# A graph layer kernel: the last stage's index words in loads of 16 registers instead of 32, and two small operations earlier in a hop's end

## The reference: two graph layers, each with a norm behind it

```python
edge_index = jnp.stack([src, dst])
x = _layernorm(x + _L0_gnn_ref(x, edge_index, edge_attr_70, Wf, bf, Wq, Wk, Wa, Wu, bu), axis=-1)
x = _layernorm(x + _L1_gnn_ref(x, edge_attr3_4x1, src, dst), axis=-1)
```

```python
def f(y):
    return jax.ops.segment_sum(y[src3] * e3, dst3, num_segments=N)
k1 = f(x)
k2 = f(x + dt * k1 / 3)
k3 = f(x + dt * (k2 - k1 / 3))
k4 = f(x + dt * (k1 - k2 + k3))
y = x + dt * 0.125 * (k1 + 3 * (k2 + k3) + k4)
```

## Time and profile before

| | |
|---|---|
| median of 3 runs | 3495.34 us |
| the profiled execution | 3501.67 us |
| its span, first to last instruction | 3499.9 us |
| busy in the span: PE, DVE, ACT, POOL | 1189.6, 2478.0, 1452.2, 2597.1 us |
| the walk's stretch, about 3096 to 3500 us: busy PE, DVE, ACT, POOL | 304.3, 126.5, 127.4, 339.7 us |
| mean granted TensorE clock, span and walk | 0.627 and 0.83 |

### The profile page before, as it was taken

The page is one execution under the profiler, slowest core; times in us unless marked ns, Lnnn a source line. Parts: engine busy times, 40 slices in busy tenths (PEclk is TensorE's granted clock), DMA queues, the critical chain, the costliest instruction groups (busy, mean ns, idle before and its releaser), DMA issues.

```text
span 3499.9 us, 31921 instructions
## 1 busy us (share of the span) xinstructions
PE 1189.6 (34%) x6041; PEld 999.4 (29%) x6041; DVE 2478.0 (71%) x6241; ACT 1452.2 (41%) x3372; POOL 2597.1 (74%) x2761
## 2 busy tenths in 40 slices
PE   4666664666661311101111101111100000047777
PEld 4555653544441211101111101111000000046776
DVE  7677616888888786657777767777769999943332
ACT  4445544666661222213333323333325555533333
POOL 7777766777757777767777767777767777748888
PEclk8777787788875555555555555555555555568888
DMA  5555585666653444436777767777757777777775
GB/s 134 172 167 176 175 174 159 217 211 213 215 193 114 147 138 151 147 121 220 252 255 241 248 202 243 247 253 254 237 180 261 263 260 259 264 215 196 197 205 142
DMA packets 423033, 710.22 MB, mean 203 GB/s; under 512 B 100050, under 2 KB 286734, under 8 KB 416592
## 3 DMA queue, kind: packets, MB, share of 16 engines
q1 hardware_dynamic: 235754, 474.50, 40.0%
q0 software_dynamic: 82128, 182.11, 19.2%
q10 hardware_dynamic: 104960, 51.58, 5.1%
HBM read 370.71 MB, written 337.25 MB: 202 GB/s over the span
## 4 chain that ended last, share of the span: by engine, by line
POOL 43%; issue 17%; DVE 14%; PE 8%; DMA 2%; ACT 2%; ACTq 0%; DVEq 0%; SPq 0%; POOLq 0%
POOL gs L1573 32%; POOL gs L834 10%; PE psum L1937 8%; DVE psum L1689 3%; DVE stats L1239 2%; DVE tn L1654 2%; DVE da L1699 2%; DVE psum L1670 2%; DVE new_res L1233 2%; ACT psum L1632 1%; DVE mv L1245 1%; DMA gs<-u,far_row 0%; PE psum L1919 0%; DVE last_z L1695 0%; DMA u<-cross,first_idx 0%
## 5 line engine op out<-in xcount | busy, mean ns | idle before, releaser
L1573 POOL DMA_INDIRECT gs<-u,far_row x1176 | 1115.4, 948 | 363.6 <-issue 357.4
L1133 PE MATMUL psum<-wu_i,d_xt 128*128 128x128 f32 (+1 forms) x782 | 210.9, 443 | 1100.0 <-DVE d_res L1165 1099.9
L1632 ACT ACTIVATE psum<-da 128x512 f32<-128x512 f32 x288 | 173.1, 601 | 888.3 <-DVE tn L1654 553.8
L1670 DVE TENSOR_TENSOR psum<-gs,psum 128x1024 f32<-128x1024 f32 x192 | 234.9, 1224 | 419.0 <-DMA gs<-u,far_row 285.1
L1133 PEld LDWEIGHTS psum<-wu_i,d_xt 128*128 128x128 f32 (+1 forms) x782 | 176.4, 326 | 1136.4 <-issue 1136.4
L343 POOL DMA_INDIRECT pt<-in_x_dram,idx x392 | 386.1, 985 | 123.6 <-issue 119.0
L834 POOL DMA_INDIRECT gs<-rows_e,edge_id x392 | 370.9, 946 | 141.4 <-issue 119.1
L1573 POOL DMA_INDIRECT gs<-x1s,far_row x392 | 374.2, 955 | 120.7 <-issue 119.1
L1689 DVE TENSOR_TENSOR_SCAN psum<-goes_on,psum 128x1024 f32<-128x1024 f32 (+1 forms) x200 | 447.5, 2238 | 0.6
L1909 DVE TENSOR_TENSOR hot<-pos,rel_s 128x1536 f32<-128x1536 f32 x66 | 125.4, 1903 | 255.3 <-ACT psum L1975 228.1
L1937 PE MATMUL psum<-ring,hot 128*128 x1584 | 292.4, 340 | 11.0 <-issue 1.6
(11 more groups left out here) (286 smaller groups left out, 3944.4 us busy)
## 6 DMA issues: line engine op xcount, KB each, us to landing
u<-da SPq DMA_DIRECT2D x144, 512.0 KB, 4.0
rows_e<-pt SPq DMA_DIRECT2D x48, 1056.0 KB, 4.7
total<-tn SPq DMA_DIRECT2D x98, 512.0 KB, 3.3
gs<-total SPq DMA_DIRECT2D x98, 512.0 KB, 5.9
fin_d<-normed SPq DMA_DIRECT2D x49, 516.0 KB, 4.9
ring<-fin_d SPq DMA_DIRECT2D x49, 516.0 KB, 4.7
gs<-u SPq DMA_DIRECT2D x49, 512.0 KB, 5.4
gs<-x1s SPq DMA_DIRECT2D x49, 512.0 KB, 6.4
```

What stands on the lines that cost most here:

```text
L1133: t = pe.matmul(d_new_psum[k % 2][0:P, r * D:(r + 1) * D], d_xt[k % 4][:, r * 128:r * 128 + P], wu_i[:, :], start=True, stop=True)
L1573: g.indirect_dma_start(gx[b % 4][:, j * D:(j + 1) * D], None, source[:, :], bass.IndirectOffsetOnAxis(ap=far_row[:, c:c + 1], axis=0)).the ...
L1632: act.mul(shared, half(us[b % 3], i), share).then_inc(shared_set, 1)
L1670: return v.tensor_tensor(zf.rearrange("p (h f) j -> p j h f", h=H), by_head(gxv(b % 4)[:, c0:c1, 0:D]), per_head(wt_rest[:, c0:c1, :] if b ...
```

## The change

There are two edits.

1. WORDS, the number of steps for each load, goes from 24 to 12. A row of `place_d` and `place_s` is then PITCH = 12 + 4 = 16 words long, and PE loads 16 registers for each 12 steps, 66 times, in place of 32 registers for each 24 steps, 33 times. The total number of words stays 1056. SP writes 66 short rows into `place_d` instead of 33 longer ones, in the same two transfers.
2. In hop 3's end, `o_shifts(v, 47)` (the last batch but one) stands ahead of `keep_last` of the last piece instead of behind `o_rows(v, 48)`.

```diff
-WORDS = 24
+WORDS = 12
+PITCH = WORDS + WORDS // 3
@@
-    place_d = nc.dram_tensor("place_d", (STEPS // WORDS, 32), I32).ap()
+    place_d = nc.dram_tensor("place_d", (STEPS // WORDS, PITCH), I32).ap()
@@
-                sp.dma_start(place_d[:, WORDS:32].unsqueeze(0), at_open.rearrange("o (g k) -> o g k", k=WORDS // 3)
+                sp.dma_start(place_d[:, WORDS:PITCH].unsqueeze(0), at_open.rearrange("o (g k) -> o g k", k=WORDS // 3)
@@
                 add_up_runs(i + 1)
+                if h == 3:
+                    o_shifts(v, b - 1)
                 keep_last(i + 1)
@@
                     o_rows(v, b)
-                    o_shifts(v, b - 1)
                     o_statistics(v, b)
@@
-        place_s = sb("place_s", [1, STEPS // WORDS * 32], I32)
+        place_s = sb("place_s", [1, STEPS // WORDS * PITCH], I32)
@@
-                        place_s[0:1, 32 * n:32 * n + 32], (mybir.EngineType.PE,), min_val=0,
+                        place_s[0:1, PITCH * n:PITCH * n + PITCH], (mybir.EngineType.PE,), min_val=0,
@@
-                        g = n * 2 + tri // TRI_OF
+                        g = n * (WORDS // GROUP) + tri // TRI_OF
```

## The result

The changed kernel takes 3503.74 us, the median of 14 runs (3500.8 to 3511.17); beside it the kernel before took 3496.19 (3492.66 to 3499.3, 14 runs). The ratio is 1.0023, with a 95% interval of 1.0016 to 1.0030: some 7.6 us slower. The prediction said 3512 and slower.

A forecast was written before the change was run, and what follows sets the result against it. PE's sequencer, not its engine, was taken to bound the walk. Loads 15.6, walk's end 1, hop's end 0 and words' transfers 0 made 16.6 us, over the median of 3495.34 3511.9, said as 3512 us; range 3494 to 3518.

The forecast's parts named there:

- What bounds the walk: In the walk, PE's sequencer sets the pace, not its engine: 11.90 us a piece, 8 x 1.18 and a load.
- The load: In PE's walk, 65 loads of 16 registers on the path in place of 32 of 32: +15.6 us.
- L32: Time of one load of 32 registers in PE's walk, taken as 2.5 us.
- L16: Time of one load of 16 registers in PE's walk, put at 1.47 us.
- the line between the two prices that were measured: PE's load price: straight from 0.50 us for one register to 2.5 for 32; 8 to 19 us added, 66 in 100.
- The rival by the register: PE's loads priced by register alone, 1.25 us for 16: +1.3 us, 3497.6 with the walk's end; 16 in 100.
- The walk's end: Behind the walk's last load, four tris may run at a low clock: up to 1.4 us, put at 1.
- break-even: In the walk, the change costs nothing if a load of 16 registers takes 1.23 us.
- The slow clock as rival: In the walk, PE's clock stays at 1.2 GHz through all four tris: 12 us on top, 3524; 8 in 100.
- The hop's end: In hop 3's end, moving `o_shifts` to the scan's end changes nothing at the statistics: 0, 0.2 us either way.
- the words' transfers: SP's two transfers into DRAM in hop 0 may double their issue time, 1.8 us uncovered; put at 0.
- Two signs named in advance: In PE's timeline, pieces of 12 steps about 6.2 us apart, and waits on "issue" of 85 to 95 us.

The follow-up runs named there:

- E7: Kernel before with each step's product over 65 of its 129 columns, the other columns of the sums left out, loads and instructions as many: ratio 1.0006.
- E3: As E1, but a load of 8 registers for each 6 steps, 132 loads: ratio 1.0035, +12 us.
- E6: As E1, but each of the 66 loads takes 32 registers, of which 16 are used: ratio 1.0252, +87 us.
- E4: Kernel before with loads of 24 registers for each 24 steps, and the tri's own word by a one-register load at each of 264 tris: ratio 1.0258, +91 us.
- E5: As E3, but a load of 4 registers for each 3 steps, 264 loads: ratio 1.0154, +53 us.
- E1: The change without the moved `o_shifts`, so only the loads of 16 registers against the kernel before: ratio 1.0025.
- E2: Kernel before with only the `o_shifts` move in hop 3's end, loads still of 32 registers: ratio 1.0002.

## Why the prediction was right, and where its size was off

**What bounds the walk: right.** The sequencer's own time does. E7 (experiment 7) leaves the time as it was with 77 us more of engine work in the walk; E3 to E6 change only the loads, with the same products, and the time follows the loads; and in the changed kernel the pieces are 4 x 1.18 us and a load. One reading was off without harm: of the two waits on `hot` in the earlier trace rows only the 5.38 us at the start are `hot`. The other one, 2.77 us at 3174.56, is a load's: its `hot` was done at 3162.9.

**The load: the sign right, the size off.** The term was 65 x 1.47 - 80 = +15.6 us. It measured 65 x 1.355 - 78.7 = +9.4. L32 was 2.46 instead of 2.5, which is +1.3. The rest is L16. The step that was mis-sized is "the line between the two prices that were measured": one end, 0.50 us for one register, was ACT's 0.58 us with a guess at what the waits and the copy's start take of it. On PE one register costs 0.33 to 0.36 us. And the line is not straight. By size, undisturbed (the shortest that come often, less 1.17) and as a mean over the walk (the mean piece less 1.18 us for each tri):

| registers | shortest common, us | mean, us |
|---|---|---|
| 1 (E4) | 0.33 to 0.36 | not separated |
| 4 (E5) | 0.38 to 0.40 | 0.51 |
| 8 (E3) | 0.65 | 0.72 |
| 16 (after; E1) | 1.14 | 1.355; 1.31 |
| 32 (before; E2) | 2.20 | 2.46; 2.42 |

The last price stands in an interval before, from the eighth tri's open to the next piece's, 3.37 - 1.17:

```profile
3337.99 0.17 PE L1919 MATMUL psum<-none 128*128 128x2 bf16 x1
...
3341.36 0.17 PE L1919 MATMUL psum<-none 128*128 128x2 bf16 x1 [2.10 <-issue]
```

Undisturbed, from 4 registers on each further one costs some 0.065 us; from 1 to 4 they are almost free. So an undisturbed load of 8 or more pays about 0.12 us beside its registers, where the line had 0.44. In the means it is more, 2 x 1.355 - 2.46 = 0.25 us by the lengths 16 and 32. The first end of the line was a least price, and I had read it as a fixed part of every load. The rule of the Trainium skill that the prediction set beside it ("DMA: Bandwidth & Descriptors", "Latency and other measured facts", a floor of some 600 ns) has the word for this, a floor; its size was not met, a load of one register on PE taking 0.33 to 0.36 us; ACT's 0.58 us, which the prediction took as agreeing with it, was an upper bound that had waits and a copy's start in it. The other rule (the Trainium skill, "Runtime: NRT & Kernel Launch", "Instruction fetch mechanics", 200 ns for each register from HBM) has the form that the price takes from 4 registers on, at a third of its size for SBUF.

**The rival by the register** (+1.3 us) was nearer in its mechanism than in its number. Half of 2.46 is 1.23 us, and the load of 16 took 1.355: 0.125 us more for each of 65 loads, 8 of the 9.4 us. That is half of what a load costs beside its registers, since half of 2.46 has half of one such part in it. The other 1.2 us is the first load, which both kernels hide and which had 32 registers before.

**How much of this was luck.** The break-even was L16 = 1.23, half of L32. By undisturbed loads alone the change adds 65 x 1.14 - 32 x 2.20 = +3.7 us, within the 7 us that the prediction called no change. The other 5.7 of the 9.4 us come with the longer kind of load, which comes at every length that was measured and which the prediction did not know. That the slowdown came out above these 7 us rests on this longer kind. It also hid part of the error: the forecast fixed part, 0.44 us, was nearly four times the 0.12 us of undisturbed loads, and the longer loads, which it left out, made up for some of the difference.

**The walk's end: right as a risk, wrong as a sum.** I put 1 us for a slow clock behind the last load. The last four tris ran at 1.18, 1.17 and 1.15 us; from the last load's open to the span's end are 12.2 us after and 17.0 before, and four tris fewer are 4.7. It cost nothing here, because the clock in these last 4.6 us was 1.00. The case that the prediction feared is in E6's profile: behind its last load the granted clock was 0.54, the tris were 1.80, 1.54 and 1.53 us apart, and from the last load's open (3571.63) to the span's end (3585.2) are 13.6 us, 1.4 more than after. So the 1 us was a price that some executions can pay, not a wrong mechanism.

**The slow clock as rival: did not come.** The granted clock in the walk rose from 0.83 to 0.88, with shorter gaps, and the pieces that had tris at the slow clock are not longer than the others: the 26 pieces after in which some tris stood 1.5 us or more apart took 5.96 us in the mean, the other 39 took 6.15. The prediction's reason against this rival does not hold in general, though: in E7 PE had hardly a gap left, and the granted clock stayed at 0.50.

**The hop's end and the words' transfers: right.** 4.43 against 4.45 us, and E2's ratio; 0.85 and 1.01 us for the issues.

**Two signs named in advance.** Pieces of 6.2 us were said, and over 6.3 for the clock, 6.0 for a price by the register: 6.075 lies between. The waits on "issue" were to grow to 85 to 95 us and fell to 62.8. That forecast forgot what the earlier trace rows had shown, that a load beside a busy engine leaves no idle time.

**Left open.** Loads and some tris come in a second length, mostly 0.2 to 0.4 us longer (0.65 and 0.90 in E3, 1.14 and 1.49 after; a few loads after are 0.6 longer); it accounts for most of the gap between the two columns of the table. What causes it was not tested. It is not random: in E5 long and short intervals alternate over most of the walk (95 of the 109 that are over 1.7 us are at every second load), and in E3 the long load comes at every fifth load from the middle of the walk on, most with a tri of 1.3 us before it. Fetches of PE's instructions can't be all of it: E5's trace has 44 packets of instructions, for all engines together, between 3096 and 3541 us. No version here beats the kernel before: loads get cheaper for each word only as they get longer, and 32 registers is the longest that was tried.

## What to carry to other kernels

Where addresses come from registers, count the sequencer's time for a piece of work, loads included, from open to open, and not the engine's idle time beside it: in this walk that idle time fell while the time rose. Few long register loads beat many short ones, but by a small fixed part (0.12 us each for undisturbed loads here, some 0.25 us in the mean), so halving a load of 32 cost 9 us over 65 loads and not the 87 that as many full loads cost. And do not lay a line through the shortest case of an operation: what it costs at size one may be a least price that longer ones do not pay on top.

## What the runs showed of the hardware that was not expected

- A register load from SBUF on PE: 0.33 to 0.36 us for one register, 0.38 to 0.40 for four, 0.65 for eight, 1.14 for sixteen, 2.20 for thirty-two, where nothing disturbs it. Only the sequencer is held; the engine goes on with what is queued: in E7 PE was busy 371 of 380 us with 2.2 to 2.5 us of load in every piece of 11.88.
- A wait of PE on the words can carry the name of DVE's `hot`: in E4 24 such waits, though `hot` was done 15 us and more before. Compare the end of the releaser with the start of what it released.
- Narrower products brought the slow clock. With 65 columns in place of 129 the granted clock was 0.50 through the walk instead of 0.83, and a tri took the engine 1.41 us where at the slow clock and 129 columns it took 1.53: half the columns saved 8%. All ten executions had it (0.59 over the whole span, 0.63 before).
